# An attention block on one core: weights transposed by VectorE, scores and values in plain float32 in 32x64 tiles

## The reference

```
xn = layernorm(x, g_in)
q = (xn @ Wq).reshape(b, n, H, DH).transpose(0, 2, 1, 3) * scale
kv = xn @ Wkv;  k, v = kv[..., :DH], kv[..., DH:]      # null key and value in front
sim = q @ k.T + bias + causal and key mask             # bias 16x128x128
out = softmax(sim) @ v                                 # heads side by side: 1024 wide
return x + layernorm(out @ Wo, g_out)
```

## Time and profile before

| | us |
|---|---|
| runs | 1216.24, 1217.46, 1217.88 |
| median | 1217.46 |
| the profiled execution | 1217.43 |
| its span, first to last instruction | 1215.6 |
| PE busy in it | 1178.6 (97%) |
| DVE / ACT / POOL busy | 980.4 / 983.9 / 828.8 |
| mean granted clock of TensorE | 0.992 |

### The profile page before, as it was taken

How to read it: one execution, slowest core, us unless ns; L and a number is a source line. 1 busy time by engine, 2 the same in 40 slices (tenths; PEclk the granted TensorE clock), 3 DMA queues, 4 the chain that set the end, 5 groups by cost and what they waited for, 6 DMA issues and landing times.

```text
span 1215.6 us, 34031 instructions
## 1 busy us (share of the span) xinstructions
PE 1178.6 (97%) x8320; PEld 1086.5 (89%) x8320; DVE 980.4 (81%) x4249; ACT 983.9 (81%) x3434; POOL 828.8 (68%) x1520
## 2 busy tenths in 40 slices
PE   4799999999999999999999999999999999999996
PEld 4699998999999999999999999999999999999994
DVE  6778888888788788888888788788888888788873
ACT  4878887888888888887888888888887888888873
POOL 2647767667677667767667677676766677677676
PEclk9899999999999999999999999999999999999999
DMA  6101111111111111111111111111111111111011
GB/s 201 54 20 55 40 53 36 36 55 54 37 54 35 37 54 55 36 54 36 36 55 54 37 52 38 37 54 55 36 53 37 36 55 54 37 50 40 19 36 53
DMA packets 39282, 58.47 MB, mean 48 GB/s; under 512 B 9792, under 2 KB 13376, under 8 KB 39104
## 3 DMA queue, kind: packets, MB, share of 16 engines
q1 hardware_dynamic: 36992, 54.81, 14.1%
q10 hardware_dynamic: 2112, 2.10, 0.5%
HBM read 40.11 MB, written 16.78 MB: 47 GB/s over the span
## 4 chain that ended last, share of the span: by engine, by line
PE 89%; POOL 3%; issue 2%; DVE 2%; ACT 1%; POOLq 0%; DVEq 0%; ACTq 0%
PE ps_proj L456 32%; PE ps_o L449 28%; PE ps_s L411 10%; PE ps_wt L421 7%; PE ps_pv L435 7%; PE ps_pv L438 3%; PE ps_proj L473 2%; POOL bias_b L863 1%; POOL w_nrm L872 1%; PE ps_proj L483 1%; POOL y_nrm L908 0%; DVE q_sb L623 0%; DVE s_low L531 0%; ACT exp_bot L744 0%; POOL y_out L912 0%
## 5 line engine op out<-in xcount | busy, mean ns | idle before, releaser
L872 POOL TENSOR_TENSOR w_nrm<-exp_bot,w_inv 128x256 f32<-128x256 f32 x256 | 157.5, 615 | 319.2 <-DVE w_inv L552 313.4
L863 POOL TENSOR_TENSOR bias_b<-bias_c,mask_add 128x256 f32<-128x256 f32 (+1 forms) x512 | 295.6, 598 | 0.1
L456 PE MATMUL ps_proj<-xt_hi,wq_hi 128*128 128x256 f32 x1024 | 290.0, 283 | 5.2 <-DVE q_sb L623 3.8
L456 PE MATMUL ps_proj<-xt_lo,wq_hi 128*128 128x256 f32 x1024 | 289.5, 283 | 0.0
L456 PE MATMUL ps_proj<-xt_hi,wq_lo 128*128 128x256 f32 x1024 | 289.3, 282 | 0.0
L796 ACT CAST q_sb<-ps_proj 64x256 fp32r<-64x256 f32 x512 | 187.7, 367 | 113.3 <-PE ps_proj L456 97.4
L623 DVE TENSOR_TENSOR q_sb<-ps_proj,q_sb 64x256 fp32r<-64x256 f32 x512 | 216.3, 422 | 25.8 <-ACT q_sb L796 14.3
L449 PE MATMUL ps_o<-wo_hi,o_hi 128*128 128x512 f32 x512 | 223.5, 437 | 0.2 <-DVE o_lo L565 0.2
L744 ACT ACTIVATE exp_bot<-logit_bot,neg_max 128x129 f32<-128x129 f32 x512 | 202.2, 401 | 10.9 <-DVE neg_max L543 6.6
L449 PE MATMUL ps_o<-wo_lo,o_hi 128*128 128x512 f32 x512 | 202.8, 396 | 0.0
L449 PE MATMUL ps_o<-wo_hi,o_lo 128*128 128x512 f32 x512 | 202.8, 396 | 0.0
(11 more groups left out here) (92 smaller groups left out, 2569.0 us busy)
## 6 DMA issues: line engine op xcount, KB each, us to landing
x_in<-in_x_dram SPq DMA_DIRECT2D x32, 512.0 KB, 3.5
x_res<-in_x_dram SPq DMA_DIRECT2D x64, 256.0 KB, 2.7
out_dram<-y_out SPq DMA_DIRECT2D x64, 256.0 KB, 2.0
w_raw<-in_L_cond_Wq_dram ACTq DMA_DIRECT2D x4, 512.0 KB, 8.1
w_raw<-in_L_cond_Wo_dram SPq DMA_DIRECT2D x4, 512.0 KB, 6.4
mask_u<-in_mask_BxS_bk_dram SPq DMA_DIRECT2D x32, 32.0 KB, 3.3
bias_c<-in_fside_16xSxS_dram SPq DMA_DIRECT2D x4, 128.0 KB, 6.9
y_nrm<-in_L_cond_Wkv_dram SPq DMA_DIRECT2D x1, 256.0 KB, 6.6
```

The costliest lines, as they stand in the source:

```text
L456: mm = pe.matmul(ps[:, 0:TOK], w[:, k, cols], xt[:, k], start=(j == 0), stop=(j == len(todo) - 1))
L863: ins = nc.gpsimd.tensor_tensor(out_, bias, key_mask, ALU.add)
L872: ins = nc.gpsimd.tensor_tensor(out_, w_exp[:, s, :, 0:keys_], w_inv[:, s, 2 * i:2 * i + 2].unsqueeze(2).to_broadcast([P, 2, keys_]), ALU. ...
```

## The change

Transposing by PE goes. POOL's weights are transposed by DVE in blocks of 32x32 (`transposed`, into `wt`), in which keys lie on partitions within a block and the four 32-row strips are two halves of the queries' strips by head. Q, keys, weights and values are kept once, in plain float32: Q is copied out of PSUM by one DVE instruction of 128x256 a part, where ACT and DVE wrote hi and lo in four instructions of 64x256. `scores_low`, `weights_t`, `weights_hi`, `weights_lo`, `keys_lo`, the transposes of v on PE and its copies go, and `ps_wt` and `s_low` with them.

Scores and values are done in visits of PE, one every second step. A visit makes the scores of two steps and half of the values of one sequence. Each contraction is cut into parts of 32 rows, each output is 64 partitions wide, so a matmul takes a tile of 32 rows x 64 columns of the array. A visit has two phases: the first uses for the scores the lower 32 rows of each 64 and for the values the upper ones, the second the other way, and accumulates on the same banks. Between the phases stands one projection of the front. The output projection is done in two halves of twelve matmuls, at steps 1 and 3 of four; heads are read for a whole sequence at once, two instructions on ACT and two on DVE in one step of four.

v is written out by ACT, spread by eight transfers of SP to four strips of partitions (`spread_v`), and transposed by one DVE instruction a group.

```diff
+PLAN = {"pv_a": 6, "pv_b": 8, "heads": 8, "out_a": 9, "out_b": 11, "stats": 12, "scale": 13, "norm": 14, "add": 15}
 FRONT = {
-    0: [("q", 7, 0)],
...
+    0: [("q", 6, 0), ("q", 7, 0)],
     1: [("x", 0, 1), ("x", 1, 1)],
+    2: [("kv", 0, 1), ("q", 0, 1)],
+    4: [("q", 1, 1), ("q", 2, 1)],
+    5: [("q", 3, 1)],
+    6: [("q", 4, 1), ("q", 5, 1)],
 }
+ITEMS = {
+    1: ([(1, 0), (1, 1), (1, 2)], [(1, 3), (0, 0), (0, 1)]),
+    0: ([(1, 0), (1, 1)], [(1, 2), (0, 0)]),
+}
 # SP
+            def spread_v(f):
+                wait(sp, v_raw_made, f + 1)
+                wait(sp, v_made, f)
+                for a in range(2):
+                    for i in range(P // BLK):
+                        sp.dma_start(v_rep[BLK * i:BLK * (i + 1), a],
+                                     v_raw[DH + BLK * a:DH + BLK * (a + 1)]).then_inc(ld_v, 16)
 # PE
+            def score(p, t, half, r):
+                for e in range(2):
+                    rows = slice(BLK * (2 * e + half), BLK * (2 * e + half + 1))
+                    scored = ps_s[e][:, 0:2 * WIDE].rearrange("p (s n) -> p s n", s=2)
+                    for u in range(2):
+                        for s, late in (((0, 1),), ((1, 1),), ((0, 0), (1, 0)))[r]:
+                            from_ = N * b + HALF * late
+                            mm = pe.matmul(scored[HALF * u:HALF * (u + 1), s, 0:N] if late else
+                                           scored[HALF * u:HALF * (u + 1), s, N:WIDE],
+                                           q_sb[rows, slot, t % CB + s, u, from_:from_ + HALF],
+                                           keys[rows, slot, b, 0:N if late else HALF], ...)
+            def values(back, part, half, r):
+                qh = 1 - half
+                late, j = ITEMS[qh][part][r]
+                for u in range(2):
+                    rows = slice(BLK * (2 * u + qh), BLK * (2 * u + qh + 1))
+                    for e in range(2):
+                        mm = pe.matmul(ps_pv[u][DH * e:DH * (e + 1), :, at:at + BLK], v32[rows, slot, b, j],
+                                       wt[rows, b, block], ...)
+            def visit(p, t, first, last, half):
+                if scoring and half == 0:
+                    wait(pe, s_read, 4 * m)
+                for batch, back, part in parts if half == 0 else ():
+                    if part == 0:
+                        wait(pe, wt_made, CB * batch + CB)
+                        wait(pe, o_lo_made, 2 * batch)
+                if half == 1:
+                    pe.wait_ge(s_half, 4 * m + 4)
+                    pe.wait_ge(pv_half, 8 * batch + 4 * part + 4)
+                for r in range(...):
+                    score(p, t, half, r)
+                    values(*todo[r][:2], half, todo[r][2])
             def body(p, first, last):      # PE
+                    parts = list(front_parts(p, t, first, last))
+                    if t % 2 == 0:
+                        visit(p, t, first, last, 0)
+                        front(parts[0])
+                        visit(p, t, first, last, 1)
+                    the other parts: front(...); then project_out(...) where it is due
             def body(p, first, last):      # DVE
+                    out_stats where due
+                    logits(n, t)
+                    inverse(n - LAG_SUM, t - LAG_SUM)
+                    heads_lo(batch, 0), heads_lo(batch, 1) where due
+                    for part in front_parts(p, t, first, last): front(*part)
+                    transposed(n - LAG_T, ...)
 # DVE
+                nc.vector.transpose(wt[:, par, :, c], w_nrm[:, s]).then_inc(wt_made, 1)
+                    nc.vector.tensor_copy(q_sb[:, slot, i // 2, i % 2], ps[:, 0:TOK]).then_inc(q_made, 1)
             def logits(n, t):
+                wait(dve, s_done, 2 * (n - s) + 4)
+                        ins = nc.vector.tensor_tensor_reduce(
+                            out_[:, e, 0:keys_], ps_s[e][:, from_:from_ + keys_], bias[:, e], -1.0, 0.0, ...)
 # ACT: heads_hi twice first in its step, then exponentials; weights_hi and the Q copies are gone
```

More of the change, by code:

```diff
@@ L390, in _, with body @@
[L390 to L395, removed]
+                if i == 1:
+                    spread_v(0)
+            for i in range(GB):
+                load_res(0, i)
+            load_x_and_mask(1, 0)
+            def body(p, first, loads, last):
+                spread_v(2 * p + 1)
+                if not first:
+                    store(p, -3, True)
+                    store(p, -2, True)
+                if not last:
+                    load_x_and_mask(p + 1, 1)
+                    spread_v(2 * p + 2)
+                if not first:
+                    store(p, -1, True)
+                if loads:
+                    load_x_and_mask(p + 2, 0)
+                store(p, 0, True)
+                if last:
+                    store(p, 1, True)
+                    store(p, 2, False)
+                    store(p, 3, False)
@@ L397, in _ @@
+            body(0, True, True, False)
+            with sp.Fori(1, PAIRS - 2) as p:
+                body(p, False, True, False)
+            body(PAIRS - 2, False, False, False)
+            body(PAIRS - 1, False, False, True)
+            for b in range(GB):
+                sp.wait_ge(stored[b], 16 * GROUPS + 16)
         @block.tensor
         def _(pe):
[L399 to L409, removed]
-                    for e in range(2):
[L411 to L434, removed]
-                    pe.matmul(ps_pv[:, :, HALF:N], v, w, start=(j == 0), stop=(j == len(todo) - 1))
-                for j, (_, v, w) in enumerate(parts):
-                    mm = pe.matmul(ps_pv[:, :, 0:HALF], v[:, slot, b], w[:, s:s + 2, 2],
-                                   start=(j == 0), stop=(j == len(parts) - 1))
-                mm.then_inc(pv_done, 1)
@@ L446, in project_out @@
+            def project_out(batch, back, part):
+                b = back % GB
+                wait(pe, o_lo_made, 2 * batch + 2)
+                if part == 0:
                     wait(pe, y_nrm_made, batch - 1)
-                todo = [(o, w, i) for i in range(2) for o, w in ((o_hi, wo_hi), (o_hi, wo_lo), (o_lo, wo_hi))]
+                todo = [(o, w, i) for i in range(OT // 2 * part, OT // 2 * (part + 1))
+                        for o, w in ((o_hi, wo_hi), (o_hi, wo_lo), (o_lo, wo_hi))]
@@ L703, in body @@
                         inverse(n - LAG_SUM, t - LAG_SUM)
-                    if done := out_batch(p, t, STEP_OUT_STATS + 1, first, last):
-                        out_mean_var(*done)
-                    if not last and t % CG == STEP_STATS + 1:
-                        x_mean_var_of(2 * p + t // CG + 2)
+                    for batch, back in due("heads", p, t, first, last):
+                        for u in range(2):
+                            heads_lo(batch, u)
+                    for part in front_parts(p, t, first, last):
+                        front(*part)
```

444 lines of the change are left out of this document (197 added, 247 removed).

## The result

The change makes the kernel slower: 1333.01 us median of 4 runs (1331.04 to 1335.95) against 1217.67, ratio 1.0952 with a 95% interval of 1.0928 to 1.0976. The forecast was 1162 us, with a chance of 0.58 for faster. The time lies above the forecast's own range (1110 to 1215), inside the wide one (1078 to 1385), and among the times of rival A (1230 to 1400), but not for rival A's reason.

The account below looks back on a forecast made before the run. PE was taken as the bound, at 36.53 us a group. Kept work 25.25, phases 6.96 and stall 2.60 sum to 34.81 us, 1.72 x 32 = 55 us less: 1162 us from 1217.4, own range 1110 to 1215.

Parts of the forecast that it names:

- the wide one: Outer range for the time, from 1078 us (stall hidden) to 1385 us (small matmuls at full 60 ns each).
- rival A: Phases bound by handing over matmuls and their weights, not columns, 60 ns each: 1382 us; chance 0.30 (1230 to 1400).
- the 11.28 us that go and the 25.25 that stay: PE's time per group: scores, weight transposes, values and v transposes removed; projections, output projection, x transposes and rest kept.
- parts 2 and 3: Visits on PE: 0.70 us a phase for small matmuls plus 0.17 for tile shape changes, 6.96 us a group.
- part 5: Other engines cost nothing, all below PE's 32 to 35 us a group; transpose 0.50 us, no margin at step 2.
- the ramp: Within a phase, 0.17 us because the first and last of the eight tiles don't start together.
- the clock leaves 1.0: Sign that the forecast is wrong: PE's granted clock falls below full; no size given.
- Part 4: PE waits for DVE's Q copy behind `o_lo`, before x and before q 3: 1.3 us each, 2.6 us a group.
- B: Small matmuls' tiles do not overlap at all, 31 us of phases a group: near 1985 us; chance 0.05.
- C: PE's stall for the Q copy doesn't show, 32.21 us a group: 1079 us; chance 0.10.
- D: Softmax chain ends last, visits at step 2 about 1 us late twice a group: 1226 us; chance 0.08.

Follow-up runs that it names:

- half-width run: Kernel after the change, its small matmuls reading only the upper 16 bits of each number as bfloat16, so results are coarse: 1135.94 us.
- The written out loop: Kernel after the change with only PE's loop over the 14 middle bodies written out, other engines keeping theirs: 1275.28 us.
- the control: Kernel before the change with PE's loop written out: 1219.54 us, ratio 1.0011.

## Why the prediction was wrong

The bound before, the 11.28 us that go and the 25.25 that stay held. The sum of 34.81 us a group failed: over twelve bodies a body of two groups takes 80.9 us, 40.5 a group. Two steps are wrong. The cost of a phase, the 0.87 us of parts 2 and 3, was mis-sized; it measured 1.18. This alone lifts the sum to 37.3 us, above the 36.53 of before, and turns faster into slower. And a wait was put at nothing that part 5 never looked for, the fetch of PE's own instructions, with the fall of the clock behind it. The 5.6 us more, in order of size:

- Parts 2 and 3, the size of a phase. I put 0.70 + 0.17 = 0.87 us; it is 1.27 and 1.10, mean 1.18: 8 x 0.31 = 2.5 us a group, 80 us in all. Four passes instead of three are 0.11 of it (0.64 for 384 columns against 0.53). The way in and out is 0.10 before the first small matmul, by my estimate some 0.1 between the last one's columns and the large matmul (the half-width phase is 0.30 long for 0.16 of columns), and 0.10 more between the first and second large one (0.22 for 0.12), 0.30 instead of 0.17. I read the way out to the first start and did not look at the second, though in the trace of the kernel before the second start behind the change comes after 0.17 us and the third after 0.11. What is left, 1.18 - 0.64 - 0.30 = 0.24 us, stands against the 0.17 of the ramp; part of it is the order of the last round of scores, which took 0.05 to 0.10 off a phase in its own experiment.
- A wait that stands nowhere in the prediction: the fetch of PE's instructions. I gave rival A the handing over of matmuls inside a phase, and did not ask how large the body becomes. The first gap at a jump is 0.97 to 1.39 us from start to start where 0.33 is due, the second 2.15 to 2.83; together they cost 3.3 us a body on average, 1.6 us a group. The written out loop shows it on one side, the control and the half-width run, in which the body is kept, on the other.
- The granted clock. Its falls to 1.2 GHz stand behind these gaps, 58 us between 100 and 1130, worth up to half of that, 1.1 us a group; "the clock leaves 1.0" was named as a sign, without a price. With the gap gone and the stalls for Q left (up to 2.4 us) it still fell five times there, with thirteen stalls of 2.2 us or more from start to start; with both gone, never.
- Part 4, the stall, was right in mechanism, place and nearly in size (82 against 83 us of idle time, released by DVE's `q_sb`, 60 times). Less the 0.12 that is due anyway, the starts stand 1.43 us apart before q 3 and 1.4 to 1.9 before x, some 0.5 us a group more than I put, since idle time leaves out the latency of the last matmul. These four terms make 2.5 + 1.6 + 1.1 + 0.5 = 5.7 us, with the clock at its upper bound.
- Part 5 was right on DVE's transposes (0.564 us against 0.50) and on the missing margin at step 2: no wait showed as long as the stall stood before it, and 24 us came in as soon as it was gone.

Rival A had the sign and nearly the size. The sign that was to tell it from the forecast, the time from the first to the last small start, came out at 0.87 and 0.77 us, between the 0.70 of the forecast and the 0.9 of A. Its cause is refuted for the rounds of 128 columns: starts stand 0.11 us apart by eights, and half the columns with as many matmuls took the rounds to 0.06. It may hold in the last round. Rivals B and C are refuted; D, the weight transposes ending last, came only once the stall of part 4 was gone. What stays open is why the last round is longer than its 0.21 us of columns (0.43, of which 0.15 lie behind its last start). The 0.22 us between the first and second large matmul are the same in the half-width run, so they do not belong to the number format.

So the dear phases made the change slower only together with the stall: with the same phases, but without stall, fetch and waits for `wt`, the kernel takes 1176 us, and in another order of the last round 1156.

## What to carry to other kernels

Before products are cut into small matmuls in a loop, count PE's instructions in its body: beyond what it keeps, each jump back fetches them again. Here bodies of 0.07 and 0.10 MB were kept and one of 0.15 was not (estimates: queue q8's bytes by the number of bodies in the program). The row of the instruction queue in the page tells it (0.21 or 3.00 MB here). Whether a body too large hurts as much where large matmuls stand behind the jump, no run shows. A projection that covers one wait is taken from the cover of another, so look at what PE has left behind the visit, and let the copy that frees PE's bank stand before work that waits for another engine.

## What the runs showed of the hardware

- Eight tiles of 32x64 on four row strips and four banks work side by side: rounds 0.11 us apart at 128 columns of plain float32, 0.06 at 64.
- A plain float32 product is two recorded matmuls, each as long as two periods of 2.4 GHz for every column (0.11 us at 128).
- A PE program with a body of some 0.07 MB is loaded once though it loops 14 times (0.21 MB in all). One with a body of 0.15 MB is fetched again at each jump back (3.00 MB), and PE's starts fall back by 2.9 to 3.6 us a turn, by 3.8 to 4.8 with the phases side by side.
- From full-size float32r matmuls to 32x64 tiles and back costs 0.10 us before the first small one, and 0.10 between the first and second large one, besides what lies between.
- Between 100 and 1130 us the clock fell 12 times in the kernel after, behind gaps of 2.1 us and more from start to start, and never in the two versions without stall and fetch, in which no gap there was above 1.8 us (1197 and 1199 us).
